# A three-part model in one program on one core: setup in two groups of constants, shorter inverse roots, expert work dealt out singly, adjacent rings of differences

## The chip, the cores and the metric

The kernel runs on one core of a Trainium2 chip. The metric is the device time of one execution in microseconds; the median of three runs of the kernel before is 4794.21 us (4791.25 to 4811.75). Compared kernels share a chip.

## What is computed

The reference has three parts in a row, over 4096 poses of 50 joints in 3 coordinates, and 4096 rows of text:

```python
# token part: 3 graph attention layers on a chain of 50 joints, widths 3 -> 64 -> 128 -> 64
for W, a_s, a_d, bg, R, g, b in layers:
    h = _gat(x, src, dst, W, a_s, a_d, bg)      # 4 heads, softmax over each joint's edges
    x = gelu(_layer_norm(h + x @ R, g, b))
x = _layer_norm(x.reshape(.., 50 * 64) @ fpW + fpb)
h = concatenate([x, txt], axis=1)
# attention part: silu, causal convolution of 4, norm of the query, memory of two matrices
h = h + _L0_attn_ref(_layernorm(h))
# expert part: 8 experts 128 -> 512 -> 128, the best two of a softmax weigh
h = h + _L0_ffn_ref(_layernorm(h))
```

The edge list is an input. The kernel checks on the chip that it is the chain of joints (each joint with itself and its neighbours) and has a second, slower branch for any other graph.

## The kernel before

The work goes in 16 steps of 256 poses (two groups of 128), one step after another, written out. Each engine has its own program, and counting semaphores with numbers worked out join them. The order on each engine is the order of the code.

A step `s` is staged over its neighbours. `iteration(s)` holds layers 1 and 2 of step `s`; `window(s + 1)` holds layer 0 of step `s + 1` together with the attention part of step `s`; the experts of step `s - 1` are spread over both, as fillers of TensorE's waits. On TensorE one step is, in order: layer 1 (26 tasks, one per four joints and group), its norm, the scores of layer 2, layer 2 (13 tasks), its norm with the pose projection, then the window.

- **A task of a layer** (`graph_layer`, L862). In round `n` TensorE does `spread_alpha(n)` (L829 or L832), `product_d(n + 1)` (L812, or L815 and L816), `own(n - 2)` (L846, L850) and `plus_neighbours(n - 2)` (L859). ScalarE copies the product (`take_d`, L1292 or L1296) and reads the result twice (`square`, L1308 and L1309). VectorE makes the differences of neighbours times the weights (`neighbours`, L1803). `product_d` has one bank and waits until the last product is copied.
- **The squares** go to a ring of six slots `SQ` (`SQN = 6`). `variance(i)` (L696) sums four tasks' squares and frees their slots: `square(n)` for `n >= 6` waits for `variance((n - 6) // 4)`. It comes in round `4 i + 6`, but the first of layer 1 in round 7, since it shares a bank with the logits.
- **A norm** (`rstd`, L1841): ScalarE copies the variances, TensorE turns them (L716), VectorE takes the inverse root in eleven operations (`rsqrt`, L1796, `newton`, L1786), splits it into three bf16 parts, TensorE turns these back (L723), ScalarE copies (L1258), and TensorE spreads them over the pairs of tasks (L736, L740). For each pair VectorE multiplies (`normalise`, L1870), ScalarE takes the gelu (L1264), and TensorE makes the scores (L759, L754).
- **An expert** has four units of `up` (L916, a hidden tile of 128 columns of weights), a gelu on ScalarE (`hidden`, L1344, into four slots `HD`) and four of `down` (L925). `hidden` of an expert's first unit waits until the `down` of the last expert is done (`eo_ps`). `add_expert` (L2019) adds the result on VectorE.
- **The start** (L404 to L1543). SP issues all constants and then the first poses; TensorE and VectorE wait for all constants (`c_loaded`). Combined weights are made, then 100 matmuls (L604) count the edges for each pair of joints in every partition, VectorE compares 2600 numbers with a constant and sets `flag`. GpSimd waits for the flag before `scores_0(0)` and `edges_0(0)`; VectorE then makes the weights of layer 0 and TensorE starts `window(0)`.
- `keep_warm` (L612) runs matmuls whose result nobody reads.

## Time and profile before

| | us |
|---|---|
| median of three runs | 4794.21 |
| the profiled execution, its own time | 4790.66 |
| its span in the trace | 4788.9 |
| TensorE busy | 4235.0 (88%) |
| VectorE busy | 3576.6 (75%) |
| ScalarE busy | 2610.1 (55%) |
| GpSimd busy | 632.2 (13%) |
| mean granted clock of TensorE | 0.970 of full |

A step in the middle of the program takes 281.0 us: in the trace L716 of layer 1 starts at 1975.0 and next at 2256.0 us. All places below are of that step unless another is named. The busy time of TensorE holds modelled ends; its waits are read from the bracket behind a row, which gives the idle time before it and who ended it.

### The profile page before, as it was taken

What the parts mean: (1) busy time and instruction counts of PE and PEld (TensorE: products, weight loads), DVE (VectorE), ACT (ScalarE), POOL (GpSimd) and SP (SyncE); (2) the same over time, 40 slices, a digit from 0 to 9 for tenths busy, and PEclk for the clock granted to TensorE, in tenths of its full rate; (3) what the DMA queues carried; (4) which work ended last, traced back from release to release, by engine and by line L of the source; (5) the groups of instructions that cost most, each with busy time, mean ns of one, the idle gap of its engine ahead of it and who ended that gap; (6) DMA issues with size and microseconds to landing.
All of it is one profiled execution on the core that took longest, in us unless ns stands there. A gap on an engine that the chain in (4) does not pass through costs nothing.

```text
span 4788.9 us, 62742 instructions
## 1 busy us (share of the span) xinstructions
PE 4235.0 (88%) x22774; PEld 1933.7 (40%) x22774; DVE 3576.6 (75%) x8027; ACT 2610.1 (55%) x3929; POOL 632.2 (13%) x746
## 2 busy tenths in 40 slices
PE   4688989899998988989998898989899898999988
PEld 4223343443434334343433434344343433434345
DVE  1677788777778877777787777788777887777772
ACT  0454656556565555656555565555556565565643
POOL 1110201111020111102011120111102011110100
PEclk9798999999999999999999999999999999999998
DMA  2000000000000000000000000000000000000000
GB/s 96 2 1 3 1 3 3 2 4 1 3 3 3 3 1 6 1 3 3 3 3 1 6 1 3 3 2 4 1 3 3 3 3 2 5 1 3 3 2 6
DMA packets 22964, 24.35 MB, mean 5 GB/s; under 512 B 3394, under 2 KB 21834, under 8 KB 22138
## 3 DMA queue, kind: packets, MB, share of 16 engines
q1 hardware_dynamic: 22650, 20.26, 1.4%
q8 instruction: 185, 3.03, 0.3%
q14 instruction: 129, 1.06, 0.1%
HBM read 16.06 MB, written 4.19 MB: 4 GB/s over the span
## 4 chain that ended last, share of the span: by engine, by line
PE 62%; DVE 22%; ACT 9%; issue 5%; POOL 1%; SPq 0%; DMA 0%; DVEq 0%; ACTq 0%; POOLq 0%
PE bank L859 11%; PE bank L812 7%; PE bank L925 7%; PE bank L916 6%; PE bank L696 4%; PE bank L829 3%; ACT X L1264 3%; PE bank L770 3%; PE bank L850 2%; PE bank L815 2%; DVE X L1870 2%; DVE Ho L2019 2%; PE bank L832 1%; PE bank L708 1%; PE bank L759 1%
## 5 line engine op out<-in xcount | busy, mean ns | idle before, releaser
L1870 DVE TENSOR_TENSOR X<-X,bank 128x1024 f32<-128x1024 f32 (+2 forms) x432 | 483.5, 1139 | 273.3 <-PE bank L736 152.1
L1264 ACT ACTIVATE X<-X,c_vec 128x1024 f32<-128x1024 f32 (+2 forms) x432 | 497.6, 1174 | 309.5 <-DVE X L1870 308.6
L1308 ACT ACTIVATE X<-bank,bgc 128x512 f32<-128x512 f32 (+1 forms) x624 | 418.6, 671 | 418.7 <-PE bank L859 416.8
L916 PE MATMUL bank<-XT,c_w 128*128 128x512 f32 x1024 | 500.1, 613 | 44.6 <-ACT SQ L1344 42.6
L925 PEld LDWEIGHTS bank<-c_w,SQ 128*128 128x128 f32 x4096 | 481.9, 192 | 56.5 <-issue 50.2
L925 PE MATMUL bank<-c_w,SQ 128*128 128x128 f32 x4096 | 500.8, 277 | 0.0
L532 POOL TENSOR_TENSOR R<-X 128x512 f32<-128x512 f32 (+1 forms) x208 | 257.2, 1240 | 1576.0 <-PE bank L812 796.4
L812 PE MATMUL bank<-R,c_W 64*128 64x512 f32 (+1 forms) x832 | 457.6, 630 | 7.6 <-ACT R L1292 2.9
L859 PE MATMUL bank<-R,c_C 128*128 128x512 f32 (+1 forms) x832 | 455.5, 629 | 0.0
L846 PE MATMUL bank<-X,WR 64*128 64x512 f32 (+1 forms) x832 | 448.8, 624 | 0.0
L1344 ACT ACTIVATE SQ<-bank,c_vec 128x512 f32<-128x512 f32 x512 | 344.8, 685 | 152.4 <-PE bank L916 143.3
L1292 ACT ACTIVATE R<-bank 128x512 f32<-128x512 f32 (+1 forms) x416 | 242.0, 582 | 319.9 <-PE bank L812 218.3
L1309 ACT ACTIVATE SQ<-bank,bgc 128x512 f32<-128x512 f32 (+1 forms) x624 | 414.7, 665 | 0.0
L1839 DVE TENSOR_TENSOR R<-R,TB 128x512 f32<-128x512 f32 (+1 forms) x416 | 330.2, 794 | 14.3
L1833 DVE TENSOR_TENSOR R<-bank,R 128x512 f32<-128x512 f32 (+1 forms) x416 | 279.2, 671 | 80.8 <-PE bank L829 50.8
L1838 DVE TENSOR_TENSOR TB<-bank,R 128x384 f32<-128x384 f32 (+1 forms) x624 | 326.4, 523 | 0.0
L916 PEld LDWEIGHTS bank<-XT,c_w 128*128 128x128 f32 x1024 | 179.6, 192 | 303.2 <-ACT SQ L1344 177.3
L829 PE MATMUL bank<-AT,sel1b 120*128 120x512 bf16 (+1 forms) x832 | 244.4, 375 | 25.5 <-DVE R L1839 16.1
L859 PEld LDWEIGHTS bank<-R,c_C 128*128 128x128 f32 x832 | 123.9, 188 | 309.4 <-issue 199.9
L859 PE MATMUL bank<-TA,c_C 128*128 128x512 f32 (+1 forms) x416 | 227.3, 628 | 0.0
L1296 ACT ACTIVATE R<-bank 128x512 f32<-128x512 f32 (+1 forms) x208 | 120.9, 581 | 190.2 <-PE bank L816 190.2
L815 PE MATMUL bank<-X,c_W 128*64 128x512 f32 (+1 forms) x416 | 207.6, 580 | 4.0 <-ACT R L1296 4.0
(257 smaller groups left out, 6853.9 us busy)
## 6 DMA issues: line engine op xcount, KB each, us to landing
c_w<-in_w SPq DMA_DIRECT2D x2, 2048.0 KB
out<-Ho SPq DMA_DIRECT2D x32, 128.0 KB, 1.9
c_fpW<-in_fpW SPq DMA_DIRECT2D x1, 3200.0 KB
X<-in_x SPq DMA_DIRECT2D x34, 75.0 KB, 2.0
X<-in_txt SPq DMA_DIRECT2D x32, 64.0 KB, 1.8
X<-in_chain SPq DMA_DIRECT2D x1, 1300.0 KB
X<-in_sel SPq DMA_DIRECT2D x1, 600.0 KB
X<-in_sel SPq DMA_DIRECT2D x1, 300.0 KB
```

The costliest lines, as they stand in the source:

```text
L812: mm(bD[:, 0:cols], W1[64 * gh:64 * gh + 64, :], DX[64 * gh:64 * gh + 64, c % 2, 0:cols], start=True, stop=True).then_inc(d_ps, 1)
L829: last = mm(b[:, 0:cols], sel1[:, c % JS, :], AT[:, sign, gh, o:o + cols], start=True, stop=True)
L846: mm(z[:, 0:cols], WR1[64 * gh:64 * gh + 64, :], X1[64 * gh:64 * gh + 64, o:o + cols], start=True, stop=False)
L859: mm(bZ[k % 2][:, 0:cols], (C1 if l == 1 else C2)[:], ta[:, 0:cols], start=False, stop=True, skip_group_check=(l == 2)).then_inc(z_ps, 1)
L916: mm(hidden_bank(e, m), w1[:, k * P:k * P + P], XT2[:], start=True, stop=True).then_inc(hid_ps, 1)
L925: last = mm(b[:, q * P:q * P + P], HD[:, m, q * P:q * P + P], w2[:, k * P:k * P + P], start=(m == 0 and q == 0), stop=(m == MT - 1), skip_ ...
L1264: A_(dst, dst, ACT.Gelu, bias=v(f"b{l}"), scale=v(f"g{l}")).then_inc(x_ok, 1)
L1308: A_(dst, bZ[k % 2][:, 0:cols], ACT.Identity, bias=bias).then_inc(zs_ok, 1)
L1309: A_(SQ[:, n % SQN, 0:cols], bZ[k % 2][:, 0:cols], ACT.Square, bias=bias).then_inc(sq_ok, 1)
L1344: A_(HD[:, m, :], hidden_bank(e, m), ACT.Gelu, bias=vec[:, FB1 + k:FB1 + k + 1]).then_inc(hid_sb, 1)
L1839: TT(ta[:, 0:cols], ta[:, 0:cols], TB[:, 0:cols], ALU.subtract).then_inc(t_ok, 1)
L1870: TT(dst, dst, b, ALU.mult).then_inc(u_ok, 1)
```

## The change

- **Start.** The constants are two groups with a semaphore each: 24 small ones first, then the first poses, then the large ones (`wq1` to `b2`, `fpW`), for which only TensorE waits, ahead of `window(0)`. The edge check makes one 50x50 matrix of counts (two matmuls), compares it with a chain built on chip, and spreads the answer with one matmul. The full count is left to the other branch. GpSimd starts `scores_0(0)` and `edges_0(0)` when the combined weights are there (`setup_sb`), ahead of the flag. TensorE runs 40 `keep_warm` after the flag.
- **Inverse root.** One operation for the first guess, one Newton step, one step of third order: eight operations, not eleven, in all seven places of a step.
- **Experts.** The first two units of `up` of experts 0 and 4 stand around the last `variance`, the first of expert 5 ahead of `variance_rows` of layer 0. In the norm of layer 1 expert 1's units stand one to a pair, and four `keep_warm` matmuls are gone; the scores come one pair later. Two units of expert 7 stand ahead of `down` of expert 6, two of expert 3 ahead of `down` of expert 2. `product_d` and `gate_rows` come ahead of `score_columns`.
- **Tokens in layer 1.** Attention norm, columns, logits, and top two come two rounds later on all engines, and with them the first `variance`, which moves from round 7 to 9.
- **Layer 2.** The first third of the next step's weights (`alphas` part 0) moves from inside layer 2 to ahead of it. The products lie in three adjacent slots and the differences in another three, so that where slots are neighbours one operation of 512 columns stands for two of 128 and 384; in layer 1 so for every odd `c`.

```diff
             for name, t in consts.items():
-                sp.dma_start(t, A[name]).then_inc(c_loaded, 16)
+                sp.dma_start(t, A[name]).then_inc(c_early, 16)
             for gh in range(GH):
                 sp.dma_start(X0[:, gh, :, :], A["x"][0, gh]).then_inc(x0_in, 16)
+            for name, t in late.items():
+                sp.dma_start(t, A[name]).then_inc(c_loaded, 16)
...
+            pool.wait_ge(setup_sb, 2)
+            scores_0(0)
+            edges_0(0)
             pool.wait_ge(flag_ok, 1)
+            nc.gpsimd.memset(Y[:].rearrange("p x a r -> p (x a r)"), 1.0).then_inc(y_pad, 1)
...
-            pe.wait_ge(c_loaded, 16 * NCONST)
+            pe.wait_ge(c_early, 16 * NEARLY)
...
+            pe.wait_ge(hot_ok, 1)
+            for t in range(2):
+                last = mm(bank[4][0:J, 0:J], HOT_S[:, t, :], HOT_D[:, t, 0:J], start=(t == 0), stop=(t == 1))
+            last.then_inc(edge_ps, 1)
+            pe.wait_ge(odd_ok, 1)
+            mm(bank[5][:, 0:1], other[0:J, 0:1].to_broadcast([J, P]), ones[0:J, 0:1], start=True, stop=True).then_inc(odd_ps, 1)
...
-                    first = 7 if l == 1 and tail else 4 + lag
-                    if n == 7 and l == 1 and tail:
+                    first = 9 if l == 1 and tail else 4 + lag
+                    if n == 9 and l == 1 and tail:
                         pe.wait_ge(lgm_ok, s)
...
+                        if done == NT[l] - 1 and tail:
+                            up(s - 1, 0 if l == 1 else 4, (0,))
                         variance(s, l, done // 4)
+                        if done == NT[l] - 1 and tail:
+                            up(s - 1, 0 if l == 1 else 4, (1,))
...
                     variance(w, 0, BATCHES[0] - 1)
+                    if moe:
+                        up(t - 1, 5, (0,))
                     variance_rows(w, 0)
...
                     up(t - 1, 6)
+                    up(t - 1, 7, (0, 1))
                     down(t - 1, 6)
...
-                    up(t - 1, 7)
+                    up(t - 1, 7, (2, 3))
...
-                    if m in (2, 3):
-                        keep_warm(2, bank[4])
...
+                    if tail and 3 <= m < 7:
+                        up(t, 1, (m - 3,))
+                    if tail and 7 <= m < 11:
+                        down(t, 1, (m - 7,))
...
+                keep_warm(40, bank[7])
                 pe.wait_ge(y_ok, 2)
                 pose_rows(0, range(4))
+                pe.wait_ge(c_loaded, 16 * NLATE)
                 window(0, True, False, False)
...
+            def rsqrt(y, v, t, done=None):
+                root = math.sqrt(3 / 8)
+                link(TS(y.bitcast(i32), v.bitcast(i32), -0.5, float(0x5f3759df), ALU.mult, ALU.add))
+                link(STT(t, y, -0.5, v, ALU.mult, ALU.mult))
+                link(TT(t, t, y, ALU.mult))
+                link(STT(y, t, 1.5, y, ALU.add, ALU.mult))
+                link(STT(t, y, root, v, ALU.mult, ALU.mult))
+                link(TT(t, t, y, ALU.mult))
+                link(STT(t, t, -1.25 / root, t, ALU.add, ALU.mult))
+                ins = STT(y, t, 1.875, y, ALU.add, ALU.mult)
...
+                    elif c % 3 < 2:
+                        last = TT(ring[:, o:o + cols], HS[:, h + P:h + P + cols], HS[:, h:h + cols], ALU.subtract)
...
+                if c % slots:
+                    link(TT(TB[:, 0:cols], am[:, 0:cols], ring[:, o - P:o + cols - P], ALU.mult))
...
-                    if moe and n == 1:
+                    if moe and n == 3:
                         attention_norm(t)
...
                 alphas_out(s, 2)
+                if nxt:
+                    alphas(s + 1, 0, F0b, M0, Al0, (0,))
                 for n in range(NT[2]):
                     neighbours(s, 2, n, True)
-                    if nxt and n in (1, 3, 6):
+                    if nxt and n in (3, 6):
```

Three places of TensorE's order. First the end of the window; L916 and L942 are `up`, L925 and L951 `down`, L1033 and L1061 the memory's second matrix, L1040 and L1068 `wout`, L795 and L817 the weights turned for layer 1. Before:

```order
L916 MATMUL bank<-XT,c_w 128x512 x4
L925 MATMUL bank<-c_w,SQ 128x128 x16
L1033 MATMUL bank<-X,c_mw 128x512 x2
L916 MATMUL bank<-XT,c_w 128x512 x4
L1040 MATMUL bank<-c_wout,X 128x128 x4
L925 MATMUL bank<-c_w,SQ 128x128 x8
L795 MATMUL bank<-identb,Pt 120x128 x32
L925 MATMUL bank<-c_w,SQ 128x128 x8
```

and with the change:

```order
L942 MATMUL bank<-XT,c_w 128x512 x6
L951 MATMUL bank<-c_w,SQ 128x128 x16
L1061 MATMUL bank<-X,c_mw 128x512 x2
L942 MATMUL bank<-XT,c_w 128x512 x2
L1068 MATMUL bank<-c_wout,X 128x128 x4
L951 MATMUL bank<-c_w,SQ 128x128 x8
L817 MATMUL bank<-identb,Pt 120x128 x32
L951 MATMUL bank<-c_w,SQ 128x128 x8
```

Two units of expert 7's `up` now stand ahead of expert 6's `down`, and two behind the memory's matrix.

Second, the rounds of layer 1 behind the logits (L907, L933); L829 or L851 opens a round, L696 and L718 are `variance`. Before:

```order
L907 MATMUL bank<-c_rw,XT 128x8 x4
L829 MATMUL bank<-AT,sel1b 128x512 x2
L812 MATMUL bank<-R,c_W 128x512
L846 MATMUL bank<-X,WR 128x512
L859 MATMUL bank<-TA,c_C 128x512
L696 MATMUL bank<-SQ,c_V 32x512 x4
L829 MATMUL bank<-AT,sel1b 128x512 x2
L812 MATMUL bank<-R,c_W 128x512
L846 MATMUL bank<-X,WR 128x512
L859 MATMUL bank<-R,c_C 128x512
L829 MATMUL bank<-AT,sel1b 128x512 x2
L812 MATMUL bank<-R,c_W 128x512
```

and with the change:

```order
L933 MATMUL bank<-c_rw,XT 128x8 x4
L851 MATMUL bank<-AT,sel1b 128x512 x2
L834 MATMUL bank<-R,c_W 128x512
L868 MATMUL bank<-X,WR 128x512
L881 MATMUL bank<-R,c_C 128x512
L718 MATMUL bank<-SQ,c_V 32x512 x4
L851 MATMUL bank<-AT,sel1b 128x512 x2
L834 MATMUL bank<-R,c_W 128x512
L868 MATMUL bank<-X,WR 128x512
L881 MATMUL bank<-TA,c_C 128x512
L718 MATMUL bank<-SQ,c_V 32x512 x4
L851 MATMUL bank<-AT,sel1b 128x512 x2
```

Before, the first batch ends round 7 and the second is three rounds off; now the first ends round 9 and the second round 10.

Third, the norm of layer 1 from the third pair on; L736 and L758 spread a pair, L759 and L781 are scores. Before:

```order
L759 MATMUL bank<-X,A 32x512 x4
L916 MATMUL bank<-XT,c_w 128x512 x2
L736 MATMUL bank<-TB,ohb 128x512 x2
L916 MATMUL bank<-XT,c_w 128x512 x2
L736 MATMUL bank<-TB,ohb 128x512 x2
L759 MATMUL bank<-X,A 32x512 x4
L736 MATMUL bank<-TB,ohb 128x512 x2
L925 MATMUL bank<-c_w,SQ 128x128 x16
L736 MATMUL bank<-TB,ohb 128x512 x2
L759 MATMUL bank<-X,A 32x512 x4
L736 MATMUL bank<-TB,ohb 128x512 x4
```

and with the change:

```order
L942 MATMUL bank<-XT,c_w 128x512
L758 MATMUL bank<-TB,ohb 128x512 x2
L942 MATMUL bank<-XT,c_w 128x512
L758 MATMUL bank<-TB,ohb 128x512 x2
L781 MATMUL bank<-X,A 32x512 x4
L942 MATMUL bank<-XT,c_w 128x512
L758 MATMUL bank<-TB,ohb 128x512 x2
L942 MATMUL bank<-XT,c_w 128x512
L758 MATMUL bank<-TB,ohb 128x512 x2
L781 MATMUL bank<-X,A 32x512 x4
L951 MATMUL bank<-c_w,SQ 128x128 x4
L758 MATMUL bank<-TB,ohb 128x512 x2
```

The expert's units came two and four at a time, and now stand one behind each pair.

## Rows read from the trace of the kernel before

**Rows 1.** Page, part 4: the chain that ended last, by engine.
```profile
PE 62%; DVE 22%; ACT 9%; issue 5%; POOL 1%; SPq 0%; DMA 0%; DVEq 0%; ACTq 0%; POOLq 0%
```

**Rows 2.** Timeline of the start (start us, duration us, engine, line, operation, count, idle before).
```profile
24.54 8.87 SPq L406 DMA_DIRECT2D X<-in_x  x2
...
39.88 0.50 DVE L1510 COPY X<-X 64x64 f32<-64x64 f32 x4 [39.88 <-DMA X<-in_chain]
...
49.10 0.29 ACT L1204 ACTIVATE identb<-c_ident 128x128 bf16<-128x128 f32 x1
...
49.44 42.91 PE L604 MATMUL bank<-SQ 74*128 74x52 f32 x200 [3.15 <-ACT identb L1204]
...
103.22 3.71 POOL L486 TENSOR_TENSOR X<-X,A0b 128x400 f32<-128x400 f32 x4
...
117.87 1.46 DVE L1581 SCALAR_TENSOR_TENSOR X<-X 128x1248 f32<-128x1248 f32 x1 [16.30 <-POOL X L509]
...
136.11 3.13 PE L676 MATMUL bank<-c_ident,X 128*128 128x128 f32 x13 [43.76 <-DVE X L1554]
```

**Rows 3.** Windows of the start: busy time by engine, granted clock, DMA share, GB/s.
```profile
0.00:16.00 16.00, 0.00 (x0) 0.00 (x0) 0.00 (x0) 1.28 (x1) 4.20 (x11) 1.00 0.52 121
136.10:159.00 22.90, 17.49 (x69) 5.56 (x69) 0.00 (x0) 12.17 (x26) 6.64 (x7) 0.64 0.03 7
```

**Rows 4.** Groups by line: count, busy us, mean ns of one.
```profile
L1308 ACT ACTIVATE X<-bank,bgc 128x512 f32<-128x512 f32 (+1 forms) x624 | 418.6, 671 | 418.7 <-PE bank L859 416.8
...
L1292 ACT ACTIVATE R<-bank 128x512 f32<-128x512 f32 (+1 forms) x416 | 242.0, 582 | 319.9 <-PE bank L812 218.3 <-DVE R L1839 74.3 <-DVE TA L1839 27.2
...
L1788 DVE SCALAR_TENSOR_TENSOR R<-TB,R 128x128 f32<-128x128 f32 x144 | 42.1, 293 | 4.9
```

**Rows 5.** Windows: one step, its first norm before and after the inverse root.
```profile
1975.00:2256.00 281.00, 255.16 (x1404) 115.25 (x1405) 222.43 (x500) 162.86 (x246) 39.44 (x46) 0.99 0.01 3
1975.00:1982.10 7.10, 7.10 (x40) 4.84 (x41) 4.42 (x16) 4.79 (x7) 0.00 (x0) 1.00 0.00 0
1982.10:2008.40 26.30, 22.16 (x132) 9.46 (x130) 18.41 (x23) 17.57 (x17) 14.13 (x22) 1.00 0.00 1
```

**Rows 6.** Timeline inside that norm.
```profile
1983.88 0.60 PE L612 MATMUL bank<-sel1b 120*128 120x512 bf16 x2
...
1987.59 1.98 PE L916 MATMUL bank<-XT,c_w 128*128 128x512 f32 x4
...
1994.17 3.73 PE L925 MATMUL bank<-c_w,SQ 128*128 128x128 f32 x32
```

**Rows 7.** Timeline of the scores and layer 2 of the same step.
```profile
2009.55 1.09 PE L781 MATMUL bank<-c_ident,X 128*128 128x128 f32 x8 [1.19 <-ACT X L1271]
...
2034.68 0.29 DVE L1821 TENSOR_TENSOR R<-R 128x128 f32<-128x128 f32 x1 [2.32 <-ACT R L1296]
...
2044.44 0.62 PE L832 MATMUL bank<-AT,sel2b 120*64 120x512 bf16 x4 [1.50 <-DVE R L1839]
...
2051.40 0.28 DVE L1837 TENSOR_TENSOR TB<-bank,R 128x128 f32<-128x128 f32 x1
...
2052.92 0.62 PE L832 MATMUL bank<-AT,sel2b 120*64 120x512 bf16 x4 [1.75 <-DVE R L1839]
```

**Rows 8.** Timeline of the norm of layer 0, next window.
```profile
2129.70 0.42 PE L723 MATMUL bank<-identb,R 128*96 128x128 bf16 x4 [1.05 <-DVE R L1852]
```

**Rows 9.** Timeline of the end of that window.
```profile
2163.71 1.28 ACT L1344 ACT_TABLE_LOAD   x1 [0.30 <-PE bank L916]
...
2165.74 1.98 PE L916 MATMUL bank<-XT,c_w 128*128 128x512 f32 x4 [1.26 <-ACT SQ L1344]
...
2170.68 1.97 PE L795 MATMUL bank<-identb,Pt 128*120 128x128 bf16 x32 [0.28 <-DVE Pt L1604]
```

**Rows 10.** Timeline of the first rounds of layer 1 after it.
```profile
2177.55 1.23 DVE L1788 SCALAR_TENSOR_TENSOR rt<-rs,rv 128x4 f32<-128x4 f32 x1
...
2181.23 0.60 PE L829 MATMUL bank<-AT,sel1b 120*128 120x512 bf16 x2 [1.15 <-DVE R L1839]
```

More of the change, by code:

```diff
@@ L1 @@
+import math
 import numpy as np
@@ L73, in build @@
         consts = {}
+        late = {}
         def const(name):
@@ L77, in const, with late_const @@
             return consts[name]
+        def late_const(name):
+            late[name] = sb("c_" + name, list(A[name].shape))[:]
+            return late[name]
         X2 = sb("X2", [P, GH, J * P])
@@ L115, in build @@
         edges, iota = setup_const("edges", i32), setup_const("iota")
-        chain_counts = setup_const("chain")
         A0b = sb("A0b", [P, DIN, 8])
@@ L177, in build @@
         GT = X1[:, 3 * NCOL:4 * NCOL]
-        HS = [R[:, k * NCOL:(k + 1) * NCOL] for k in (0, 1, 4)]
+        HS = R[:, 3 * NCOL:6 * NCOL]
         TB = sb("TB", [P, NCOL])
@@ L396, in build @@
         block = ctx.enter_context(nc.Block())
-        NCONST = len(consts)
+        NEARLY, NLATE = len(consts), len(late)
         @block.sync
@@ L1080, in iteration @@
                 if tail:
-                    up(t, 0)
-                    down(t, 0, (0, 1))
+                    up(t, 0, (2, 3))
+                    down(t, 0, (0,))
                 else:
@@ L1086, in iteration @@
                 if tail:
-                    down(t, 0, (2,))
+                    down(t, 0, (1, 2))
                     hidden_done(t, 0)
@@ L1098, in iteration @@
                         added(t, 0)
-                    if tail and m == 11:
+                    if tail and m == 13:
                         added(t, 1)
-                    if m >= 2 and (m % 2 == 1 or m == PAIRS[1] + 1):
-                        scores(s, 1, (m - 2) // 2)
-                    if tail and m == 3:
-                        up(t, 1, (0, 1))
-                    if tail and m == 4:
-                        up(t, 1, (2, 3))
-                    if tail and m == 6:
-                        down(t, 1)
-                score_columns(s, 2)
+                    if m >= 5 and m % 2 == 1:
+                        scores(s, 1, (m - 5) // 2)
+                    if tail and 3 <= m < 7:
+                        up(t, 1, (m - 3,))
+                    if tail and 7 <= m < 11:
+                        down(t, 1, (m - 7,))
+                for i in range(PAIRS[1] // 2 - 1, BATCHES[1]):
+                    scores(s, 1, i)
                 product_d(s, 2, 0)
@@ L1271, in scores_out @@
                 A_(SC[:, 1, :], bank[4][:], ACT.Copy).then_inc(sr_sb, 1)
+                if gates is not None:
+                    gate_out(gates)
                 act.wait_ge(s_ps, s * 2 + l)
@@ L1320, in graph_layer @@
                         square(s, l, n - lag)
-                    if l == 1 and n == 5 and tail:
+                    if l == 1 and n == 7 and tail:
                         token_columns(s - 1)
-                    if l == 1 and n == 9 and tail:
+                    if l == 1 and n == 11 and tail:
                         token_weights(s - 1)
@@ L1511, in _ @@
             last.then_inc(raw_ok, 1)
+            dve.wait_ge(en_ok, 1)
+            for t in range(2):
+                TS(HOT_S[:, t, :], iota[0:EH, 0:J], EN[:, t:t + 1], None, ALU.is_equal)
+                last = TS(HOT_D[:, t, :], iota[0:EH, :], EN[:, 2 + t:3 + t], None, ALU.is_equal)
+            last.then_inc(hot_ok, 1)
+            TT(CHAIN, ident[0:J, 0:J], ident[0:J, 1:J + 1], ALU.add).then_inc(en_ok, 1)
+            dve.wait_ge(en_ok, 2)
+            TT(CHAIN[:, 1:J], CHAIN[:, 1:J], ident[0:J, 0:J - 1], ALU.add).then_inc(en_ok, 1)
             dve.wait_ge(setup_ps, 1)
@@ L1794, in newton @@
                     ins.then_inc(done, 1)
-            def rsqrt(y, v, t, done=None):
-                link(TS(t.bitcast(i32), v.bitcast(i32), 1, None, ALU.logical_shift_right))
-                link(TS(y.bitcast(i32), t.bitcast(i32), -1.0, float(0x5f3759df), ALU.mult, ALU.add))
-                for k in range(3):
-                    newton(y, v, t, done if k == 2 else None)
             def neighbours(s, l, n, chain):
@@ L2099, in iteration @@
                         add_expert(t, 0)
-                    if moe and m == 8:
+                    if moe and m == 11:
                         add_expert(t, 1)
```

145 lines of the change are left out of this document (72 added, 73 removed).

## Prediction

> **What bounds the kernel now.** I read the chain that ended last first [rows 1]: TensorE holds 62% of it, VectorE 22%. Then the windows of one step [rows 5]: TensorE is busy 255 of 281.0 us. So a step can be shortened only where TensorE waits or where it runs filler, and a saved operation elsewhere counts only if it ends such a wait. Then the start [rows 2], which no step hides: nothing computes until 39.88 us, when the last constant lands, 43 us of tiny matmuls count edges, GpSimd begins the first scores at 103.22, VectorE at 117.87 takes them up, and TensorE begins layer 0 at 136.11.
>
> **The start.** The shapes of the 24 small constants make 2.0 MB. In the first 16 us the chip moved 121 GB/s x 16 us = 1.94 MB [rows 3], and an issue takes SP under half a microsecond while its queue is not full, so I put the landing at 17 us. From there the old distances hold. ScalarE's last setup copy ended at 49.39, which is 9.5 us after 39.88: 26.5. GpSimd now waits for that, not for the flag: 103.22 to 117.87 is 14.65 us, so VectorE starts at 41.2. From 117.87 to 136.11 is 18.24 us, so TensorE starts layer 0 at 59.4, 76.7 us earlier [rows 2]. What could take it back: the large constants gate TensorE ahead of `window(0)`, but all constants together landed by 39.88, 20 us ahead of need; the flag (two matmuls, a 50x50 compare, one more matmul) is done at about 28 and hides behind GpSimd; 40 filler matmuls cost 9 us (0.21 each) to 18 us (at the lower clock) and hide behind VectorE until 59. The first poses are behind the small constants only. Before, their issue was stuck for 8.87 us [rows 2]; if they land as late as then, about 35 us, GpSimd starts 9 us later and the gain is 68. I take **76.5**, from 68 to 78.
>
> TensorE ran `window(0)` at a granted clock of 0.64 [rows 3], between its levels of 1.2 and 2.4 GHz, after 43.76 us without work [rows 2]. The new wait behind the filler is 15 to 22 us; I count on no warmer start. The Trainium skill, TensorE: Matmul & The Clock Gate, Part 1, has the clock follow how busy the array has just been; this trace agrees.
>
> **A step, place by place** (steady steps, gain positive).
>
> *First rounds of layer 1.* VectorE reaches the first task after an inverse root of 128x4 whose operations cost 0.2 us each and one 1.23 beside GpSimd [rows 10]. Three fewer give 0.6, and 1.6 if the slow one is among them; TensorE's wait there is 1.15 [rows 10]. I take **+1.1** (0.5 to 1.6). The attention norm comes two rounds later, where VectorE is no further ahead by much: 0.
>
> *The first variance.* It stood in round 7 and stands in round 9. `square(6)` needs its slot from it, and its task is ready in round 8. ScalarE must therefore stand until round 9 is over, then do the two reads of 0.67 each and the copy `take_d(10)` of 0.58 [rows 4], which overlap by 0.1: TensorE's `product_d(11)` waits 1.9 us, of which its `spread_alpha` fills 0.5. A new wait, **-1.4** (-2 to 0), in each step with tokens. Behind ScalarE's stalled square also stand VectorE's task 10, two rounds ahead of need, and the next square.
>
> *Inverse roots.* Each is three operations shorter, 0.29 and a gap of 0.03 each: 0.9 us [rows 4]. In the norms of layers 1 and 2 TensorE is busy all the while, 7.10 of 7.10 us [rows 5], since expert work fills it. That work is only moved: two of its units go to the waits around the last variance, and what is shortened comes back as a wait ahead of L723, or as `down` in front of the spread. **0** for both (-1 to +1 together). In layer 0 TensorE waits 1.05 us for VectorE [rows 8]; expert 5's unit ahead of `variance_rows` costs 0.3 of the 0.9. **+0.6**.
>
> *Norm of layer 1.* 26.3 us, of which TensorE is busy 22.16 [rows 5], 1.2 of these with the four fillers (0.60 a pair [rows 6]). I laid the new order out by hand: 0.5 a spread, 1.0 a score batch, 0.95 an `up` unit (1.98 for two), 0.93 a `down` unit (3.73 for four) [rows 6], with VectorE and ScalarE at 1.16 to 1.2 a pair. TensorE then waits 0.6 us for `added(0)`, 0.5 for pairs, 0.9 for `added(1)`, and is done after 23.9. **+2.4** (0.5 to 4).
>
> *Scores to layer 2.* `product_d` and `gate_rows`, about 1.6 us by the units above, now stand in a wait of 1.19 [rows 7]: the scores' chain is 0.3 later. Expert 3's first two units ahead of expert 2's `down` move the end of that `down` by 0.9, and expert 3's gelu needs it; its table load is then late by as much as TensorE had gained. **+0.1** (-1 to +1).
>
> *Layer 2.* TensorE waits 1.50 and 1.75 us for VectorE, which at those points does parts of the next step's weights between tasks [rows 7]. The first part, 1.2 us, moves to where VectorE sat idle 2.32 us [rows 7]: covered, and if that idle time were gone it would cost its 1.2. With the merged operations VectorE comes to the reciprocal 1.7 us earlier; the wait of 1.50 goes, and some 0.2 of that of 1.75. A merge saves at most the small operation, 0.28 [rows 7], and at least nothing; I take 0.1 by the gap between starts, 16 merges in layer 2. From task 7 on TensorE is the bound. **+1.7** (1 to 3). The Trainium skill, VectorE: DVE Perf Modes, section on the TRN2 errata, gives each instruction that reads SBUF a fixed cost, which it puts between 58 and some 150 cycles; by it a merge saves 0.06 to 0.16 us, an estimate from that page, and the sum would stay within this term's range. In layer 1 the merges hide: TensorE is the bound there.
>
> *End of the window.* The costliest line against the change. Expert 7's first two units (1.9 us) go ahead of expert 6's `down`, so the memory's matrix ends 1.9 later. ScalarE copies it, and only then loads the gelu table, 1.28 [rows 9], and does the first unit, whose slot TensorE needs for the third `up`. Before, the load began at 2163.71 behind the unit's own matmul and TensorE waited 1.26 [rows 9]. Now it waits for copy, load and unit, 2.6 us, with nothing between. L795, which had only 0.28 us of slack against VectorE [rows 9], is late by 1.6 - 0.3. **-1.4** (-2.5 to 0).
>
> Sum: 1.1 - 1.4 + 0.6 + 2.4 + 0.1 + 1.7 - 1.4 = **3.1 us** a step; with the ends of its terms against each other -2 to +7.
>
> **The total.** Steps 1 to 14: 14 x 3.1 = 43. Step 0 has no experts that cover the three shorter roots: 3 x 0.9, plus 1.7 in layer 2 and 0.6: 5. Step 15 has no next weights, but the norm of layer 1 and a tail in which VectorE's chain ends with four short roots of 0.6: 3. With the start 76.5 + 43 + 5 + 3 = 127.5. The profiled execution took 4790.66, 1.8 beyond its span; the median of the runs is 3.5 us above it. 4790.66 - 127.5 = 4663, and with part of that distance **4665 us**.
>
> **Rivals.**
> A, the forecast: the start as a whole, steps of 1 to 6 us: 4790.66 - 76.5 - 8 - (14 to 84) = 4622 to 4692. Chance 0.62.
> B, the losses eat the steps: the two new waits are longer than laid out, or the norm of layer 1 gives only its fillers. For it: both waits are certain by the order, and their cost was taken from a trace in which ScalarE ran ahead. Against it: waits of 3.4 us exist in layer 2 and go. Steps of -1.5 to +1: 4692 to 4732, about 4710. Chance 0.2.
> C, the steps give more: the shifts remove ScalarE's and TensorE's small waits in the norm, and the root shows in two more places. 6 to 9 us a step: 4580 to 4622, about 4605. Chance 0.1.
> D, the start does not move as said, since another input gates it (poses, flag), and VectorE begins above 60 us: gain 55, the rest as in A: about 4686. Chance 0.04; it lies inside the range.
> E, slower than before: the clock. With the fillers gone from the norm of layer 1 and a blank wait of 2.6 us at the end of each window, TensorE falls to 1.2 GHz in one of the two. At half clock the norm's 22 us of TensorE work would last up to 20 us longer: 15 x 20 - 84 = +216, about 5000. It decides from 5.6 us a step on (84 / 15). For it: the clock did fall between its levels in `window(0)` [rows 3]. Against it: that norm ran at 1.00 with waits of 4 us in it [rows 5], and the new one has 3. Chance 0.04.
>
> The measurement of this kernel tells about 0.5%, 24 us. Faster 0.95: A to D all pass it by the start alone. Same 0.02, slower 0.03. The range is 4612 to 4722: A, most of B, a piece of C.
>
> **What will show it.** In the changed kernel's trace: VectorE's first root chain (L1581 before) at 41, TensorE's first pose transpose at 59, a step of 278. ScalarE's L1308 with a wait of some 3.5 us once a step and TensorE's product behind it; TensorE's `up` at the end of a window with a wait of 2.6 for ScalarE in place of 1.26; no wait of 1.5 in layer 2; the norm of layer 1 at 24 us. The prediction is wrong if the step is outside 275 to 283, or if TensorE's start of layer 0 is past 70.

## The result, and the profile after

The changed kernel takes **4637.49 us**, median of 4 runs (4629.41 to 4643.92), against 4793.99 for the kernel before, 4 runs (4791.25 to 4811.75). The ratio is 0.9665, 95% interval 0.9637 to 0.9693: faster by 3.4%. Forecast were 4665 us and a range of 4612 to 4722. The profiled execution took 4643.92 us with a span of 4642.1.

The page of the changed kernel, its parts 1 and 4 (busy time by engine; the chain that ended last):

```profile
PE 4199.4 (90%) x22568; PEld 1907.3 (41%) x22568; DVE 3448.4 (74%) x7239; ACT 2593.5 (56%) x3929; POOL 627.7 (14%) x746
...
PE 69%; DVE 16%; ACT 9%; issue 5%; POOL 1%; SPq 0%; DMA 0%; DVEq 0%; ACTq 0%; POOLq 0%
```

TensorE holds more of the chain than in [rows 1], VectorE less. The start of the changed kernel, its timeline:

```profile
18.23 1.44 PE L600 MATMUL bank<-X 64*128 64x8 f32 x6 [18.23 <-DMA X<-in_iota]
...
27.43 0.29 ACT L1236 ACTIVATE identb<-c_ident 128x128 bf16<-128x128 f32 x1
...
27.86 3.69 POOL L499 TENSOR_TENSOR X<-X,A0b 128x400 f32<-128x400 f32 x4 [23.13 <-ACT identb L1236]
28.45 11.21 PE L634 MATMUL bank<-sel1b 120*128 120x512 bf16 x40 [1.36 <-ACT identb L1236]
...
42.48 1.46 DVE L1621 SCALAR_TENSOR_TENSOR X<-X 128x1248 f32<-128x1248 f32 x1 [15.20 <-POOL X L522]
...
60.72 3.13 PE L698 MATMUL bank<-c_ident,X 128*128 128x128 f32 x13 [21.06 <-DVE X L1594]
```

These rows stand against [rows 2]: the small constants land at 18.23 instead of all at 39.88, the flag's work hides behind ScalarE's copies, GpSimd begins at 27.86, VectorE at 42.48, TensorE with layer 0 at 60.72 instead of 136.11. That is 75.4 us, and the first matmuls last 3.13 us in both kernels, so the clock starts no colder. The table of counts for the edge check, 1.3 MB, is no longer loaded either.

A step is best measured from layer 1's first variance transposes (L716 before, L738 after) to the same row of the next step. Over steps 1 to 14 its mean was 283.1 us before (279.7 to 286.5; the 281.0 of [rows 5] was a short one) and is 279.3 now (275.8 to 280.4). It has three stretches:

| stretch, steps 1 to 14 | holds | before, us | now, us |
|---|---|---|---|
| layer 1's transposes to layer 2's | norm of layer 1, scores, layer 2 | 107.4 to 109.0, mean 107.8 | 103.2 |
| layer 2's to layer 0's | norm of layer 2, start of layer 0 | 41.7 to 43.0, mean 42.4 | 40.6 to 42.2, mean 41.5 |
| layer 0's to layer 1's | norm of layer 0, end of the window, layer 1 with its first variance | 130.6 to 134.5, mean 133.0 | 132.0 to 136.3, mean 134.6 |

So the first stretch gives 4.6 us a step, the second 0.9, and the third, where both new waits stand, takes 1.6 back. The span's 146.8 us are the start 75.4, step 0's layer 0 2.0, step 0 to 1 10.6, steps 1 to 14 53.5 (3.8 each) and the tail 5.4. The changed kernel also runs fillers in the first window's layer 0 (`keep_warm(2)`, before only in windows with expert work), and its granted clock is 0.78 from 60.7 to 83.7 us, against 0.64 in [rows 3]; no run separates the two, so what made the 2.0 is not shown.

The three places that the prediction named, timeline of the changed kernel: the norm of layer 1 (its waits), TensorE at the end of the window, and the round of the moved variance; the ACT rows are ScalarE ahead of the `up`.

```profile
1881.30 0.60 PE L758 MATMUL bank<-TB,ohb 96*128 96x512 bf16 x2 [0.53 <-DVE X L1919]
1882.33 1.12 PE L942 MATMUL bank<-XT,c_w 128*128 128x512 f32 x2 [0.43 <-DVE Ho L2068]
...
1899.18 2.34 PE L781 MATMUL bank<-X,A 128*32 128x512 f32 x20 [1.03 <-DVE Ho L2068]
1901.45 0.64 PE L837 MATMUL bank<-X,c_W 128*64 128x512 f32 x1
...
2057.81 0.60 ACT L1435 ACTIVATE X<-bank 128x512 f32<-128x512 f32 x1 [3.09 <-PE bank L1061]
2058.42 1.28 ACT L1378 ACT_TABLE_LOAD   x1
2059.72 1.27 ACT L1378 ACTIVATE SQ<-bank,c_vec 128x512 f32<-128x512 f32 x2
2060.46 3.42 PE L942 MATMUL bank<-XT,c_w 128*128 128x512 f32 x4 [2.69 <-ACT SQ L1378]
...
2100.67 0.69 PE L834 MATMUL bank<-R,c_W 64*128 64x512 f32 x1 [1.40 <-ACT R L1326]
```

The norm runs from its first spread at 1878.19 to `product_d` at 1901.45: 23.3 us against 26.3 [rows 5]. TensorE waits 2.69 for ScalarE's copy, table load and first unit, and then the two units behind it (x4 in the row) last 3.42 us, where the same two took 1.98 [rows 9]: the granted clock was 0.73 from 2059 to 2063, 0.84 in the next 4 us, and 1.00 after. At 2100.67 it waits the 1.40 that the moved variance was said to cost; ScalarE stands at L1342 for `variance` 15 times, 71.5 us in all, 4.8 a time and not 3.5. In layer 2 the wait of 1.50 [rows 7] is now 0.31, the other is still 1.56, and TensorE's wait of 1.15 in layer 1's first rounds [rows 10] is gone.

### The profile page after: what moved, and what is told of

It reads as the page before. It is cut to its first block, busy times and chain, and to the rows that moved or that the text cites. A ratio compares the mean times of both kernels' runs of the same rounds, so it can differ in the third digit from the quotient of the medians.

```text
span 4642.1 us, 61543 instructions
## 1 busy us (share of the span) xinstructions
PE 4199.4 (90%) x22568; PEld 1907.3 (41%) x22568; DVE 3448.4 (74%) x7239; ACT 2593.5 (56%) x3929; POOL 627.7 (14%) x746
## 4 chain that ended last, share of the span: by engine, by line
PE 69%; DVE 16%; ACT 9%; issue 5%; POOL 1%; SPq 0%; DMA 0%; DVEq 0%; ACTq 0%; POOLq 0%
PE bank L881 12%; PE bank L834 9%; PE bank L951 8%; PE bank L942 8%; PE bank L718 5%; PE bank L851 3%; PE bank L792 3%; PE bank L872 2%; PE bank L837 2%; PE bank L781 2%; PE bank L730 2%; PE bank L868 2%; DVE X L1919 2%; PE bank L854 2%; DVE Ho L2068 2%
## 5 line engine op out<-in xcount | busy, mean ns | idle before, releaser
L1342 ACT ACTIVATE X<-bank,bgc 128x512 f32<-128x512 f32 (+1 forms) x624 | 418.9, 671 | 495.9 <-PE bank L881 424.4
L942 PE MATMUL bank<-XT,c_w 128*128 128x512 f32 x1024 | 536.7, 638 | 88.6 <-ACT SQ L1378 80.2
L951 PEld LDWEIGHTS bank<-c_w,SQ 128*128 128x128 f32 x4096 | 488.1, 192 | 89.3 <-issue 70.0
L951 PE MATMUL bank<-c_w,SQ 128*128 128x128 f32 x4096 | 510.0, 277 | 0.0
L1888 DVE TENSOR_TENSOR R<-R,TB 128x512 f32<-128x512 f32 (+1 forms) x416 | 339.5, 816 | 14.4
L942 PEld LDWEIGHTS bank<-XT,c_w 128*128 128x128 f32 x1024 | 178.6, 195 | 325.9 <-ACT SQ L1378 199.6
L851 PE MATMUL bank<-AT,sel1b 120*128 120x512 bf16 (+1 forms) x832 | 244.2, 375 | 0.0
L1881 DVE TENSOR_TENSOR TB<-bank,R 128x512 f32<-128x512 f32 x320 | 217.9, 681 | 0.0
```

Of the source, the lines that this page charges most:

```text
L851: last = mm(b[:, 0:cols], sel1[:, c % JS, :], AT[:, sign, gh, o:o + cols], start=True, stop=True)
L942: mm(hidden_bank(e, m), w1[:, k * P:k * P + P], XT2[:], start=True, stop=True).then_inc(hid_ps, 1)
L951: last = mm(b[:, q * P:q * P + P], HD[:, m, q * P:q * P + P], w2[:, k * P:k * P + P], start=(m == 0 and q == 0), stop=(m == MT - 1), skip_ ...
L1342: A_(dst, bZ[k % 2][:, 0:cols], ACT.Identity, bias=bias).then_inc(zs_ok, 1)
L1888: TT(ta[:, 0:cols], ta[:, 0:cols], TB[:, 0:cols], ALU.subtract).then_inc(t_ok, 1)
```

## The experiments

The columns are the median in us, the ratio to the kernel before on the same chip with its 95% interval, and the difference to the changed kernel run again, in us: the difference of the two ratios times 4790. Apart from start_only each kernel is the changed one with the edit named; the diffs are cut to the lines that carry it. Where an undone edit also moves the clock, its time is more or less than its waits, so the stretches of the step are given beside it.

```
changed_again     4633.07  0.9686 (.9667-.9705)     0
tokens_back       4627.87  0.9666 (.9650-.9682)   -10 +-12
up7_back          4611.43  0.9640 (.9624-.9656)   -22 +-12
both_back         4587.20  0.9592 (.9576-.9609)   -45 +-12
start_only        4715.76  0.9854 (.9832-.9876)   (-70 +-10 to the kernel before)
old_root          4666.59  0.9744 (.9731-.9757)   +28 +-11
old_norm          4699.12  0.9806 (.9793-.9819)   +57 +-11
split_again       4649.70  0.9726 (.9703-.9749)   +19 +-14
alphas_back       4652.31  0.9702 (.9676-.9729)    +8 +-16
up3_back          4635.88  0.9673 (.9648-.9699)    -6 +-15
filled            4589.45  0.9584 (.9558-.9610)   -49 +-15
both_and_filled   4546.91  0.9489 (.9472-.9507)   -94 +-12
```

**The changed kernel again.**

> The changed kernel as it is, so that the three others are compared on the same chip. Both theories: 4630 to 4645 us, 0.966 of the kernel before, a step of 279 us on the mean.

4633.07 us. It gives the base for what follows.

**The two new waits.** The first variance goes back to round 7, and with it the tokens' work on all engines (norm, columns, logits, top two) two rounds earlier; expert 7's early units go back behind the memory's matrix; and then both.

```diff
-                    first = 9 if l == 1 and tail else 4 + lag
+                    first = 7 if l == 1 and tail else 4 + lag
...
                     up(t - 1, 6)
-                    up(t - 1, 7, (0, 1))
                     down(t - 1, 6)
...
-                    up(t - 1, 7, (2, 3))
+                    up(t - 1, 7)
```

> The changed kernel with the tokens' work in layer 1 where it stood before (attention norm in round 1, logits in round 6, first variance in round 7). Theory 1 (the shift costs more than it gives): ScalarE's stall at the seventh square and TensorE's wait of 1.40 us for the copy go, a wait of about 0.67 for the attention norm comes back; 0.7 to 1.4 us a step less, 10 to 21 us less in all, about 4622. Rival (the shift was what let the first rounds run without waits): the first rounds of layer 1 get back waits of 1.15 and 0.67 us, and the time is 5 to 10 us more, about 4645.

> The changed kernel with all four units of expert 7's up behind the memory's matrix, as before. Theory 1: TensorE's wait for ScalarE at that place falls from 2.69 to 1.26 us and the granted clock no longer falls behind it (the two up units took 3.42 us for 1.98), so 1.4 to 2.8 us a step less, 20 to 40 us in all, about 4608. Rival (the wait is hidden by VectorE's chain to the weights of layer 1, which ends at the same time): no more than 5 us less, 4632 or above.

> Both of these edits undone in the changed kernel. Theory 1: their gains add, 2.1 to 4.2 us a step, 30 to 60 us less in all, about 4590. Rival: the sum of two small effects, 4630 to 4645.

4627.87, 4611.43 and 4587.2 us. TensorE's waits, of the changed kernel again, of the first edit and of both (line waited for, us in all, times, longest), and the end of the window with the second edit:

```profile
PE bank L942 <- ACT SQ L1378: 80.1, 47, 2.7
...
PE bank L834 <- ACT R L1326: 29.9, 44, 1.7
```

```profile
PE bank L834 <- ACT R L1326: 3.4, 17, 0.2
```

```profile
PE bank L942 <- ACT SQ L1377: 58.9, 46, 1.5
```

```profile
2044.81 1.98 PE L942 MATMUL bank<-XT,c_w 128*128 128x512 f32 x4 [1.26 <-ACT SQ L1377]
```

Each edit takes away its own wait, 26.5 and 21.2 us of it. The second gives 22 us alone: the wait is 1.26 again and the matmuls behind it last 1.98, as before the change. The first gives 10 +-12 alone, not told from nothing and less than its wait: in its trace TensorE's busy time rose by 7.5 us with the same matmuls, at a lower clock (0.964 on the mean, against 0.967). Together the two give 45 us, 3.0 a step (3.3 by the mean step, 276.0 against 279.3): the prediction had 1.4 and 1.4. The rival, that both moves together are neutral, is out; that the first alone costs time is shown only on top of the second.

**The start alone.** The kernel before with the new start and nothing else.

```diff
-            dve.wait_ge(c_loaded, 16 * NCONST)
+            dve.wait_ge(c_early, 16 * NEARLY)
...
             with pe.If(graph == 0):
+                keep_warm(40, bank[7])
                 pe.wait_ge(y_ok, 2)
                 pose_rows(0, range(4))
+                pe.wait_ge(c_loaded, 16 * NLATE)
```

> The kernel before with the new start alone (two groups of constants, the small check of the edges, GpSimd no longer behind the flag, 40 filler matmuls); steps, roots and differences stay as they were. Theory: the start is worth the 75.4 us by which TensorE began layer 0 earlier in the changed kernel's trace, and nothing behind it moves: 75 us under the kernel before, 0.984 of it, some 4710. Rival: the early start disturbs what follows (colder clock in the first window, pose transposes queued): 60 to 70 us, above 4715. Second rival: part of what I put down to the steps (step 0 to 1 was 14.6 us shorter, most of it one drop of the clock) belongs to the start: 85 us or more, below 4702.

4715.76 us. By the ratio that is 70 us (60 to 80) under the kernel before, by the medians of this comparison 75.8 (4791.61 before). The time alone doesn't tell the theory's 75 from the first rival's 60 to 70. The trace does: TensorE begins layer 0 at 60.81, 75.3 us earlier than before, the span is 4712.8 against 4788.9, 76.1 less, and the mean step is 283.1 as before. The clock of the first window is colder, 0.57 from 60 to 83 us, but layer 0's transposes still come 22.8 us after its start, against 23.1 before. So nothing of the start is lost later, and the second rival, that part of the steps' gain belongs to it, is out too.

**The inverse root.** Eleven operations again.

```diff
-                link(TS(y.bitcast(i32), v.bitcast(i32), -0.5, float(0x5f3759df), ALU.mult, ALU.add))
-                ...
+                link(TS(t.bitcast(i32), v.bitcast(i32), 1, None, ALU.logical_shift_right))
+                link(TS(y.bitcast(i32), t.bitcast(i32), -1.0, float(0x5f3759df), ALU.mult, ALU.add))
+                for k in range(3):
+                    newton(y, v, t, done if k == 2 else None)
```

> The changed kernel with the inverse root of eleven operations again. Theory (the prediction's terms): covered in the norms of layers 1 and 2, 0.6 us a step in layer 0, some more in step 0 and the tail: 10 to 15 us over the changed kernel. Rival 1: covered everywhere, within 4 us of it. Rival 2: on the path in all three layers, 2.7 us a step: 43 us over it, 4676.

4666.59 us, 28 over. The size lies between the theory and rival 2, but the places are rival 2's. TensorE's waits for VectorE's last operation of the inverse root (L1901 or L1902), of the changed kernel again and of this one, and the norm of layer 2 in this one's timeline:

```profile
PE bank L745 <- DVE R L1901: 24.9, 32, 2.4
```

```profile
PE bank L745 <- DVE R L1902: 68.0, 48, 3.3
...
PE bank L851 <- DVE R L1889: 10.9, 15, 0.8
```

```profile
1992.33 0.42 PE L745 MATMUL bank<-identb,R 128*96 128x128 bf16 x4 [1.46 <-DVE R L1902]
...
2071.43 1.98 PE L942 MATMUL bank<-XT,c_w 128*128 128x512 f32 x4 [2.69 <-ACT SQ L1378]
```

The waits grew by 43.1 us over 48 norms, 0.9 in each: 0 to 0.85 in layer 1, 0.54 to 1.46 in layer 2, 0.99 to 1.91 in layer 0. And 0.7 came back in layer 1's first rounds, 15 times. That is 54 us of waits for a loss of 28 (20 between the two profiled executions). The rest came back as clock: TensorE was busy 4156.6 us here and 4201.7 in the changed kernel with the same 22568 matmuls, the mean granted clock is 0.978 against 0.967, and the `up` behind the wait of 2.69 lasts 1.98 here, not 3.42.

**The norm of layer 1.**

```diff
-                    if m >= 5 and m % 2 == 1:
-                        scores(s, 1, (m - 5) // 2)
-                    if tail and 3 <= m < 7:
-                        up(t, 1, (m - 3,))
+                    if m >= 2 and (m % 2 == 1 or m == PAIRS[1] + 1):
+                        scores(s, 1, (m - 2) // 2)
+                    if tail and m == 3:
+                        up(t, 1, (0, 1))
```

> The changed kernel with the old order in the norm of layer 1: expert 1's units two and two with its whole down product at pair 6, four fillers, scores a pair earlier, added(1) at pair 11, gate rows behind the score columns. Theory as predicted: 2.4 us a step, 15 steps: 36 us over the changed kernel, about 4669. Reading of the two traces: from layer 1's first to layer 2's first variance the changed kernel takes 103.2 us and the kernel before 107.3; the variance's stall adds 1.4 and the first rounds give 1.1, so the norm gave 4.4: 66 us, about 4699. Rival: what was gained there came from the roots and the units around the last variance, which stay: under 15 us.

4699.12 us, 57 over, 3.8 a step: nearer to the reading of the two traces than to the predicted 2.4. But that reading counted the variance's stall and the first rounds in a stretch in which they don't stand, and not all of the 57 is the norm. The edit holds the order behind the scores too (columns, `product_d`, gates). The stretch from layer 1's to layer 2's transposes is 106.4 us, against 103.2: the norm, from its first spread to the end of its scores, takes 26.2 instead of 23.3, and from there to layer 2's first spread it is 23.6 instead of 23.3. That is 2.9 and 0.3 a step. The step's mean grew by 4.0, and the rest is clock in layer 0's stretch (136.3 on the mean, against 134.8). TensorE's waits in this norm:

```profile
1898.84 1.06 PE L781 MATMUL bank<-X,A 128*32 128x512 f32 x8 [0.76 <-ACT X L1297]
...
1902.61 1.98 PE L942 MATMUL bank<-XT,c_w 128*128 128x512 f32 x4 [0.36 <-ACT SQ L1379]
...
1913.16 1.06 PE L781 MATMUL bank<-X,A 128*32 128x512 f32 x8 [0.62 <-ACT X L1297]
...
1915.59 0.60 PE L758 MATMUL bank<-TB,ohb 96*128 96x512 bf16 x2 [0.82 <-DVE X L1923]
```

The scores a pair later and one unit a pair remove these small waits, and what is left is 0.53, 0.43 and 1.03 (rows above). The prediction had laid them out as 0.5, 0.6 and 0.9.

**The merged differences and products.** The same rings and addresses, but two operations in every task.

```diff
-                elif c % 3 < 2:
-                    last = TT(ring[:, o:o + cols], HS[:, h + P:h + P + cols], HS[:, h:h + cols], ALU.subtract)
+                else:
+                    x = (c + 1) % 3 * NCOL
+                    TT(ring[:, o + cols - P:o + cols], HS[:, x:x + P], HS[:, h + cols - P:h + cols], ALU.subtract)
+                    last = TT(ring[:, o:o + cols - P], HS[:, h + P:h + cols], HS[:, h:h + cols - P], ALU.subtract)
```

> The changed kernel with the same rings and addresses, but the differences and products that cross a task's edge split into two operations in each task again, as before. Theory as predicted: VectorE is late in layer 2's first tasks, the merges take off some 1.5 us a step: 22 us over the changed kernel, about 4655. Rival: in the changed kernel's trace layer 2 still holds waits of 1.42 and 1.56 us, so the merges gave nothing that reaches the end of the layer: within 5 us of it. Rival 2: they count in layer 1 too, over 3 us a step: 45 us or more.

4649.7 us, 19 over (5 to 33): the interval holds the theory's 22 and does not tell it from rival 1's 5; rival 2's 45 is out. The trace is sharper. VectorE issues 448 instructions more and is busy 3470.3 us instead of 3448.1, so a merge saves 0.05 us, half of the 0.1 that I took and just under the 0.06 to 0.16 of the prediction's estimate; TensorE's wait at L854 for VectorE is 38.3 us instead of 32.0, which is 0.4 a step, and the stretch is 103.7 us in nearly every step instead of 103.2.

**The first part of the weights, and expert 3's units.**

```diff
-                if nxt:
-                    alphas(s + 1, 0, F0b, M0, Al0, (0,))
...
-                    if nxt and n in (3, 6):
+                    if nxt and n in (1, 3, 6):
```

> The changed kernel with the first part of the next step's weights back between layer 2's tasks 1 and 2 on VectorE. Theory (what is left of the prediction's 1.7 us for layer 2 once the merges have shown 1.2 of it): 0.5 us a step, 5 to 12 us over the changed kernel. Rival 1: the part's whole 1.2 us shows in TensorE's wait for VectorE: 18 us over it. Rival 2: covered at either place, within 4 us of it.

```diff
                     expert_bias(t)
-                    up(t, 3, (0, 1))
                     pe.wait_ge(s_sb, s * 2 + 2)
                     down(t, 2)
-                    up(t, 3, (2, 3))
+                    up(t, 3)
```

> The changed kernel with all four units of expert 3 behind expert 2's down product again. Theory (the prediction's small term): the early units end that product 0.9 us later and cover as much of a wait, so within 5 us of the changed kernel. Rival: as with expert 7, an early unit is a loss, since the third unit waits for ScalarE (1.46 us in the changed kernel's trace): undone it gives 0.5 to 1 us a step, 8 to 15 us under the changed kernel.

4652.31 us, 8 over, and 4635.88, 6 under: neither is told from no change by its time. The first is settled by the trace. Its timeline in layer 2, and that of the kernel with split operations and the part still moved:

```profile
1938.60 0.62 PE L854 MATMUL bank<-AT,sel2b 120*64 120x512 bf16 x4 [1.44 <-DVE R L1888]
...
1946.88 0.62 PE L854 MATMUL bank<-AT,sel2b 120*64 120x512 bf16 x4 [1.55 <-DVE R L1888]
```

```profile
1932.90 0.62 PE L854 MATMUL bank<-AT,sel2b 120*64 120x512 bf16 x4 [0.37 <-DVE R L1885]
...
1941.38 0.62 PE L854 MATMUL bank<-AT,sel2b 120*64 120x512 bf16 x4 [1.76 <-DVE R L1885]
```

1.44 stands where the changed kernel has 0.31 and the kernel without merges 0.37, and the stretch is 104.3 us, not 103.2. So it was the moved part, not the merges, that took the wait of 1.50 away; the merges took 0.2 off the wait behind it (1.76 to 1.56). The moved part gives 1.1 a step there. The mean step grows by 0.8 when it is undone (280.1, against 279.3), since the clock gives some of it back in layer 0's stretch (133.7 on the mean, against 134.8). For expert 3 the stretch is 103.2 with either order: early or late units are even.

**Fillers against the clock.** Most of the changed kernel's steps last 280.0 to 280.4 us and some 275.8, with the same work. Windows of two stretches of the changed kernel run again, of a long and a short step, which begin at layer 0's transposes (window; length; busy time and count of PE, PEld, DVE, ACT, POOL; granted clock; DMA share; GB/s):

```profile
2296.70:2312.70 16.00, 13.78 (x83) 7.47 (x81) 12.10 (x26) 8.50 (x12) 0.00 (x0) 1.00 0.00 0
2312.70:2324.70 12.00, 10.24 (x47) 4.29 (x46) 5.29 (x14) 6.42 (x8) 0.00 (x0) 0.58 0.00 1
...
2576.70:2592.70 16.00, 13.78 (x83) 7.47 (x81) 12.06 (x26) 8.46 (x12) 0.00 (x0) 1.00 0.01 1
2592.70:2604.70 12.00, 10.14 (x63) 4.65 (x60) 6.68 (x19) 7.29 (x12) 0.00 (x0) 0.86 0.00 0
```

The first 16 us are alike to 0.01 us on TensorE. Then three short waits come in both, and in one stretch the mean clock of 12 us is 0.58 and 47 matmuls are recorded, in the other 0.86 and 63. These means mix the two levels. Narrower windows show that the clock falls to half in both, for 10.2 us in one and 3.4 in the other, and that it did so in the kernel before (last row):

```profile
2314.60:2324.80 10.20, 9.55 (x44) 4.25 (x43) 3.40 (x12) 4.57 (x6) 0.00 (x0) 0.50 0.01 2
...
2597.90:2601.30 3.40, 3.40 (x16) 0.62 (x8) 1.52 (x10) 0.60 (x1) 0.00 (x0) 0.50 0.00 0
```

```profile
2426.10:2436.30 10.20, 9.55 (x43) 4.26 (x43) 3.88 (x15) 4.55 (x6) 0.00 (x0) 0.50 0.00 0
```

The waits, timeline of the longer one:

```profile
2312.26 0.62 PE L762 MATMUL bank<-TB,ohb 96*64 96x512 bf16 x4 [0.37 <-DVE X L1919]
2313.99 0.62 PE L762 MATMUL bank<-TB,ohb 96*64 96x512 bf16 x4 [1.11 <-DVE X L1919]
2315.26 1.94 PE L776 MATMUL bank<-X,A 128*32 128x512 f32 x8 [0.65 <-ACT X L1296]
```

```diff
+                    if moe and m in (4, 5):
+                        keep_warm(2 * m - 6, bank[0])
                     if m < PAIRS[0]:
                         spread_rstd(w, 0, m)
+                    if moe and m == 5:
+                        keep_warm(2, bank[0])
```

> The changed kernel with eight filler matmuls (0.21 us each at full clock) in three short waits of TensorE in the norm of layer 0 (0.37, 1.11 and 0.65 us): two ahead of the spread of pair 4, four ahead of that of pair 5, two ahead of the second batch of scores. The same 30 us of matmuls there took 4.3 us longer in one step of the changed kernel than in another, with the same waits and a granted clock of 0.5 for some 10 us in the longer one. Theory: those short waits let the clock fall, the fillers hold it, and each step takes the 275.8 us of the short ones: 3 us a step, 40 to 50 us under the changed kernel. Rival 1: the clock falls anyway, here or at the next wait: within 5 us of it. Rival 2: the fillers only delay: 0.3 to 1 us a step over it.

4589.45 us, 49 under. The same place in this kernel, windows and timeline:

```profile
2557.30:2569.30 12.00, 11.74 (x73) 5.58 (x70) 8.23 (x27) 8.44 (x14) 0.00 (x0) 1.00 0.00 1
```

```profile
2557.51 1.04 PE L634 MATMUL bank<-sel1b 120*128 120x512 bf16 x4
2558.59 0.62 PE L762 MATMUL bank<-TB,ohb 96*64 96x512 bf16 x4
2559.15 0.60 PE L634 MATMUL bank<-sel1b 120*128 120x512 bf16 x2
2559.87 1.06 PE L776 MATMUL bank<-X,A 128*32 128x512 f32 x8
```

Eight fillers in waits that were there anyway keep the clock at 1.00. The same 12 us, from 16 us behind layer 0's transposes, have 1.00 in all 13 windows 2 to 14 of this kernel; in the changed kernel they have 0.58 to 0.86 in 12 of the 13, and in the kernel before, from 17 us on, in 11 of 13. TensorE's busy time falls from 4201.7 to 4170.5 us with 112 more matmuls recorded, and the mean granted clock of the run rises from 0.967 to 0.981. The steps are 274.2 to 277.8, with a mean of 276.0; falls of 3.4 us remain elsewhere, as from 2582.0 us on. The theory holds; both rivals are out. Since the fall was there before the change, this gain is one that the change left open, and not the undoing of a loss.

**The best version.**

> The first variance at round 7 and expert 7's early units undone (both_back) and the eight fillers in the norm of layer 0, together. Theory 1 (the two gains add): 46 us by the one and 45 by the other under the changed kernel, some 4545. Theory 2 (part of what both_back gave was the clock, and the fillers hold the same stretch): the step of both_back had one step with 129.4 us where the others had 131.0 from layer 0 to layer 1, so the fillers give 1.6 us a step there, 24 us: some 4563. Rival: the fillers find no fall to hold in this kernel's steps: 4587 as before, or up to 10 us over it.

4546.91 us, 0.9489 of the kernel before (0.9472 to 0.9507), and by the ratios 94 us (82 to 106) under the changed kernel run again, where the two gains alone are 45 and 49. They add; theory 2, an overlap that would leave some 70, is out. Its steps are 271.7 to 274.9, and its stretch of layer 0 is 127.9 to 128.2.

## Why the prediction was right, and where its steps were not

The result is 27.5 us under the forecast, inside its range, by the mechanism of the forecast (rival A).

- *The start*, 76.5: 75.4 in the trace; the run with it alone gives 70 (60 to 80) by its ratio and 76.1 by its span. The landing was at 18.23, not 17, and both distances behind it held. Right, and rival D is out.
- *The first variance* and *the end of the window*, -1.4 each: waits of 1.40 and 2.69, as laid out, and 3.0 a step together when both are undone. Right in mechanism and sum; undone alone, the first variance is not told from nothing, so its own 1.4 is shown as a wait and not as time. ScalarE's stall ahead of it was laid out as 3.5 us and is 4.8. At the window's end the wait was sized rightly at 2.6, but not the two units behind it, 3.42 instead of 1.98.
- *Inverse roots*, "0 for both" in layers 1 and 2: wrong. The step that failed is "TensorE is busy all the while, 7.10 of 7.10 us": a window without idle time before the change does not say that a shorter chain is worth nothing, because the same diff took two of the expert's units out of that window. With the old root the waits are 0.85 and 1.46 there. From before to after, with the moved units in, the way from a norm's transposes to its first spread went from 7.13 to 6.80 us in layer 1, from 7.22 to 6.08 in layer 2 and from 9.05 to 8.07 in layer 0: that is 1.5 in the two layers that were put at 0, and 1.0 in layer 0, not 0.6. In the first rounds the wait of 1.15 went, as said. In sum the root gives 1.9 a step by the run, against 1.7 with the first rounds counted in. That the size came out right is luck: with the old root the places cost 3.6 a step, and the clock took back half.
- *Norm of layer 1*, +2.4: 3.0 by its window, and 2.9 by that of the run that undoes it; the 3.8 of that run's time holds 0.3 from the order behind the scores and the clock. Mis-sized, by 0.6: the small waits for ScalarE that rival C named are gone.
- *Scores to layer 2*, +0.1: 0.3 by the stretch of the run with the old norm and order, and nothing from expert 3's units.
- *Layer 2*, +1.7: 1.1 for the moved part of the weights and 0.4 for the merges, by the waits. The prediction had the merged operations bring VectorE early enough for the wait of 1.50, and the moved part as covered; it was the other way about.
- *Rival B* fell, since the norm gave more than its fillers. *Rival E* fell in its size: there was no 20 us at half clock in a step past the first. But its cause is real on a smaller scale, since both the loss behind the 2.69 wait and the different lengths of a step are clock. The prediction asked about the clock only in the first window, in the norm of layer 1 and at the window's end. In 11 of 13 steps of the kernel before it also fell behind layer 0's waits, and no term has that.
- *The step*, 278 and not outside 275 to 283: 279.3. The gain was 3.8 a step instead of 3.1, from a mean of 283.1 rather than the 281.0 of the step that I had read. The mark of 278 was thus missed by 1.3 for its base, though the gain was larger; that it stayed inside 275 to 283 says little about the terms.

The undone parts sum to 70 + 28 + 57 + 19 + 8 - 45 - 6 = 131 us, against 150 by the ratio of the changed kernel run again. The rest, 19, is within the intervals of the parts; 6 of it go if the start is taken by its span. The units around the last variance and ahead of layer 0's rows, and the fillers of the first window, were not undone by themselves, and what they are worth stays open. So does how the clock divides among the parts, since each edit moves where it falls.

## What to carry to other kernels

A window in which an engine never waits tells what a shorter input is worth only as long as the work in that window stays; if the same change moves work out of it, lay the chain out again. Work moved ahead of something that another engine waits for is no free cover: ask what that engine does next with it, here a copy, a table load and the unit whose slot TensorE wants. Where steps of identical work have two lengths, read the granted clock in windows of a few microseconds and put filler into the waits ahead of its fall: eight small matmuls gave 1% here, as much as undoing both losing moves of this change. A mean clock of 0.86 over 12 us was a short fall to half and not a higher level, so narrow the window until it shows 0.50 or 1.00. And when one part is undone, read its own stretch beside the total time: the total holds what the clock does elsewhere.

## What the runs showed that I had not expected

The granted clock falls to half around three waits as short as 0.37, 1.11 and 0.65 us with one group of matmuls between each two, for 3.4 us in one step and 10.2 in another with the same sequence. A longer wait elsewhere can thus cost less than its length, since where the clock falls moves with it: the kernel with the old root had 54 us more of waits, and lost 28. The Trainium skill, TensorE: Matmul & The Clock Gate, Part 1, has the clock follow how busy the array has just been; the fillers, which change only that, agree. Why the fall is short in one of two equal stretches and long in the other no view here shows; it stays open.

A switch of ScalarE's table costs 1.28 us for the load, with the next ACTIVATE at 2059.72 right behind its end at 2059.70, and nothing ahead of it (the copy ends at 2058.41). The Trainium skill, ScalarE: Activation LUTs, section on what ACT_TABLE_LOAD costs, adds a drain and comes to about 2.66 us; by it TensorE's wait at the window's end would have been 1.4 us longer. That is an estimate from the page; the trace does not show the drain.
